# Indirect transfers of a gated cross-attention kernel, issued without their limit-check operand

## The chip, the cores and the metric

The kernel runs on one core of one Trainium2 chip. The metric is the device time of one execution in microseconds (us). The kernel before takes 6575.31 us, the median of three runs (6571.84 to 6575.43).

The core has five engines that run side by side: TensorE (PE in the profile, its weight loads PEld), VectorE (DVE), ScalarE (ACT), GpSimd (POOL) and SyncE (SP), which here issues most of the DMAs. A small q behind a name (POOLq) is the instruction queue of that engine: its register moves, branches and waits.

## The reference

Four layers, each x = x + tanh(gate) * attention(layernorm(x)) and then x = x + tanh(gate) * ffn(layernorm(x)), over 2048 tokens of width 256, with a context of 1601 rows. What matters here are the three places in which rows are picked by computed numbers.

```python
# layer 0, attention: 16 heads, 5 sample points for each; offsets are computed from the query
loc_x = jnp.mod(ref + off + loc, sign_lens[:, None, None, None])
x0 = jnp.floor(ix)
i0 = x0.astype(jnp.int32)          # first of two neighbouring context rows
i1 = i0 + 1
sk = 0.5 * (w0 * _gather_pad0(Kh, i0) + w1 * _gather_pad0(Kh, i1))
sv = 0.5 * (w0 * _gather_pad0(Vh, i0) + w1 * _gather_pad0(Vh, i1))
# softmax over the 5 points, weighted sum of sv
...
# layers 2 and 3, ffn: top 2 of 8 experts for each token (layer 2 adds a shared expert)
sel_w, sel_idx = jax.lax.top_k(routing, TOP_K)
acc = acc + we[:, None] * _ffn(xf, w1, b1, w2, b2)
```

## The kernel before, in words

The tokens lie in 16 tiles (NT) of 128 rows (P), one token for each partition. The kernel is a list of stages; at the end of a stage its engines wait for each other, which the traces show as a drain on line 2207. A stage placed "beside" another with POOL skipped runs on the other four engines only, while POOL is still in a longer one.

**Layer 0, attention.** A stage writes a table (`kv_table`) of 26,624 rows of 64 floats: for a context row and a head, the keys and values of this row and of the next one. Another computes, for each token, 80 table rows (NO = 16 heads x 5 points). The function `gather` (line 1315) then fetches one tile: 80 indirect DMAs (line 1319), each with 128 numbers, one for each partition, so 128 rows of 256 bytes. All are issued by POOL. VectorE works on a tile when its 80 transfers have landed (lines 1257 to 1279, some 22 us a tile).

- Tiles 0 to 8 (`stage_sample_early`): POOL gathers into two buffers in turn, `s_got` and `got_late`. Tile t waits until VectorE has freed the buffer of tile t - 2 (line 1271 frees it). The copy of the next tile's numbers (line 1354) stands ahead of each tile. Beside it the other engines build keys and values for the later layers, quantize weights, scan masks, and sample the tiles.
- Tiles 9 to 15 (`stage_gather_late`): POOL gathers a tile into `got_late`, waits for it, stores it to DRAM (`late_rows`, line 1391, a plain DMA from POOL), and waits for the store. Beside it the other engines carry tiles 0 to 7 through two feed-forward layers and one attention. Then `stage_sample_late` loads the seven tiles back (`m_got`) and samples them.

So line 1319 is executed 16 x 80 = 1280 times.

**Layers 2 and 3, experts** (`stage_expert_ffn`, twice). VectorE computes for each token the two places (`place_i`) of its copies in expert order. POOL scatters the normed rows to `slots_in` (line 2150; 16 tiles x 2 copies = 32 indirect DMAs for each of the two layers). SP waits for all 32 (line 1868) and loads slots of 256 rows with the weights of their expert (lines 1870 and 1871); TensorE computes each slot. Layer 2 has a shared expert, computed on TensorE (lines 1929 and 1937) ahead of the slots. When all is stored, POOL fetches the results (line 2158, again 32 for each layer, four tiles ahead), and VectorE adds them up (lines 2139 and 2141).

The numbers are computed so that they lie inside their tables; no row is skipped in the kernel before. The limit is given as a constant; the program puts it into a register of POOL, with one MOVE ahead of each indirect transfer, under the same line.

Of the kernel before, what the change touches and what calls it, by code (L numbers as in the profile page):

```python
# [23 lines left out]
H = 16  # L24
# [3 lines left out]
MPAD = MT * P  # L28
# [7 lines left out]
SLOT = 256  # L36
SLOTS = 2 * S // SLOT + E - 1
# [1277 lines left out]
def gather(env, pool, got, numbers, arrived):  # L1315

    import concourse.bass as bass
    for j in range(NO):
        pool.indirect_dma_start(out=got[:, j, :], out_offset=None, in_=env.table,  # L1319
                                in_offset=bass.IndirectOffsetOnAxis(ap=numbers[:, j:j + 1].bitcast(env.u32), axis=0),  # L1320
                                bounds_check=MPAD * H - 1, oob_is_err=False).then_inc(arrived, 16)


def sample_buffers(env, keep):
# [8 lines left out]
def stage_sample_early(env, keep, scratch):  # L1333
# [13 lines left out]
    def gpsimd(pool):  # L1347
        pool.sem_inc(got_free, 2)
        pool.tensor_copy(numbers[0][:, :], env.rows[:, 0, :]).then_inc(copied, 1)

        def tile(t, k):
            pool.wait_ge(got_free, t + 1)
            pool.wait_ge(copied, t + 1)
            pool.tensor_copy(numbers[(k + 1) % AHEAD][:, :],
                             env.rows[:, bass_ds(t + 1, 1), :].rearrange("p o n -> p (o n)")).then_inc(copied, 1)
            gather(env, pool, got[k % 2], numbers[k], gathered[k % 2])
        with pool.Fori(0, EARLY // AHEAD, 1) as it:
            for k in range(AHEAD):
                tile(it * AHEAD + k, k)
        for t in range(EARLY // AHEAD * AHEAD, EARLY):  # L1360
            tile(t, t % AHEAD)
# [11 lines left out]
def stage_gather_late(env, keep, scratch):  # L1373

    ahead = scratch.enter_context(env.nc.sbuf_tensor("l_ahead", [P, NO], env.i32))
    zeros = scratch.enter_context(env.nc.sbuf_tensor("l_zeros", [P, NO], env.i32))
    copied, taken, zeroed = env.sem("l_copied"), env.sem("l_taken"), env.sem("l_zeroed")
    gathered, kept = env.gather_sem("l_gathered"), env.gather_sem("l_kept")

    def gpsimd(pool):  # L1380
        pool.memset(zeros[:, :], 0).then_inc(zeroed, 1)
        pool.wait_ge(zeroed, 1)
        pool.tensor_copy(ahead[:, :], env.rows[:, EARLY, :]).then_inc(copied, 1)
        with pool.Fori(0, NT - EARLY, 1) as j:
            pool.wait_ge(copied, j + 1)
            pool.tensor_tensor(env.numbers[:, :], ahead[:, :], zeros[:, :], env.ALU.add).then_inc(taken, 1)
            pool.wait_ge(taken, j + 1)
            pool.tensor_copy(ahead[:, :], env.rows[:, bass_ds(j + (EARLY + 1), 1), :].rearrange("p o n -> p (o n)")).then_inc(copied, 1)
            gather(env, pool, env.got_late, env.numbers, gathered)
            pool.wait_ge(gathered, j * (16 * NO) + 16 * NO)  # L1390
            pool.dma_start(env.late_rows[bass_ds(j * P, P), :], env.got_late[:, :, :].rearrange("p n c -> p (n c)")).then_inc(kept, 16)
            pool.wait_ge(kept, j * 16 + 16)
    return {"pool": gpsimd}
# [387 lines left out]
def stage_expert_ffn(env, keep, scratch, n):  # L1781
# [8 lines left out]
    def sb(name, shape, dt=f32):  # L1790
        return scratch.enter_context(nc.sbuf_tensor(f"e{n}_{name}", shape, dt))

    def sem(name):
        return env.sem(f"e{n}_{name}")
# [11 lines left out]
    FETCH = 4  # L1806
# [11 lines left out]
    place_f, place_i, part = sb("place_f", [P, 2, NT]), sb("place_i", [P, NT, 2], env.i32), sb("part", [P, NT, 2])  # L1818
# [7 lines left out]
    scattered = env.gather_sem(f"e{n}_scattered")  # L1826
# [4 lines left out]
    fetched, mixed = [env.gather_sem(f"e{n}_fetched{k}") for k in range(FETCH)], sem("mixed")  # L1831
# [312 lines left out]
    def gpsimd(pool):  # L2144
        pool.iota(slot_no[:, :], [[1, SLOTS]], base=0, channel_multiplier=0, allow_small_or_imprecise_dtypes=True).then_inc(iota_made, 1)  # L2145
        pool.wait_ge(*ln["y"])
        pool.wait_ge(placed, 1)
        for t in range(NT):
            for k in range(2):
                pool.indirect_dma_start(out=env.slots_in, in_=env.Y[:, t, :], in_offset=None,  # L2150
                                        out_offset=bass.IndirectOffsetOnAxis(ap=place_i[:, t, k:k + 1].bitcast(env.u32), axis=0),
                                        bounds_check=SLOTS * SLOT - 1, oob_is_err=False).then_inc(scattered, 16)
        pool.wait_ge(all_stored, 1)
        for t in range(NT):
            if t >= FETCH:
                pool.wait_ge(mixed, 2 * (t - FETCH) + 2)
            for k in range(2):
                pool.indirect_dma_start(out=got[t % FETCH][:, k, :], out_offset=None, in_=env.slots_out,  # L2158
                                        in_offset=bass.IndirectOffsetOnAxis(ap=place_i[:, t, k:k + 1].bitcast(env.u32), axis=0),
                                        bounds_check=SLOTS * SLOT - 1, oob_is_err=False).then_inc(fetched[t % FETCH], 16)  # L2160

    return {"pe": tensor, "act": scalar, "dve": vector, "sp": sync, "pool": gpsimd}

# [167 lines left out]
```

## Time and profile before

| | |
|---|---|
| median of three runs | 6575.31 us (6571.84 to 6575.43) |
| span of the profiled execution | 5943.9 us |
| difference of the two | 631.4 us |
| indirect transfers | 1280 (L1319) + 64 (L2150) + 64 (L2158) = 1408 |
| POOL busy | 1506.2 us, 25% of the span |
| PE busy | 3795.9 us, 64% of the span |

The span goes from the first to the last instruction of the profiled execution. A time of its own for that execution isn't given beside the span; what the runs take beyond it is the 631.4 us of the table, and lies outside what the trace shows.

### The profile page before, as it was taken

The page shows a single profiled execution, that of the slowest core. Times are in us where ns is not written, and L with a number is a line of the kernel's source. Part 1 is how long each engine was busy: PE and PEld are TensorE (multiplying, and loading weights), DVE is VectorE, ACT ScalarE, POOL GpSimd, SP SyncE. Part 2 cuts the span into 40 slices and gives each one's busy share as a digit, 9 for nine tenths or more (in the row PEclk, how much of TensorE's full clock was granted, in tenths as well). Part 3 has the DMA queues.
Part 4 walks back from the last instruction along what each step waited for, and adds up shares of the span by engine and source line. Part 5 has one row for each costly group of instructions (what it writes and reads, how often), then busy time and mean ns, then how long its engine had stood idle before and what let it go on. Part 6 is the DMA issues. An engine that isn't in the chain of part 4 may idle for free.

```text
span 5943.9 us, 71309 instructions
## 1 busy us (share of the span) xinstructions
PE 3795.9 (64%) x19888; PEld 1731.9 (29%) x19894; DVE 2791.6 (47%) x3817; ACT 1990.8 (33%) x3720; POOL 1506.2 (25%) x1461
## 2 busy tenths in 40 slices
PE   7700410037962013996599969974899999997695
PEld 2300200022321001332133336862222222222485
DVE  3131221276753276776566630013766666673201
ACT  1100100014751001673155621212366666664131
POOL 0767777677767400000000010010000000000202
PEclk9555655557986555998699979986799999999698
DMA  2331311013321211110211111534100111101243
GB/s 83 90 118 24 108 38 24 21 55 106 92 93 39 92 66 48 51 51 20 81 52 47 42 60 65 192 137 117 43 25 25 32 33 33 33 25 32 110 181 135
DMA packets 195461, 403.88 MB, mean 68 GB/s; under 512 B 46405, under 2 KB 130649, under 8 KB 186074
## 3 DMA queue, kind: packets, MB, share of 16 engines
q1 hardware_dynamic: 147114, 323.79, 17.0%
q0 software_dynamic: 48112, 77.16, 4.6%
q8 instruction: 122, 2.00, 0.1%
q14 instruction: 113, 0.93, 0.1%
HBM read 301.77 MB, written 106.10 MB: 69 GB/s over the span
## 4 chain that ended last, share of the span: by engine, by line
PE 47%; POOL 20%; DVE 10%; issue 10%; DMA 7%; ACT 2%; SPq 1%; POOLq 1%; DVEq 1%; ACTq 0%; PEldq 0%
POOL got_late L1319 13%; PE PS L694 13%; PE PS L657 9%; PE PS L675 8%; POOL s_got L1319 6%; PE PS L1959 5%; PE PS L1969 5%; DVE a_maxima L789 3%; ACT a_probs L745 1%; DMA q_parts<-a_parts 1%; PE PS L1929 1%; DMA late_rows<-got_late 1%; PE PS L1937 1%; PE PS L1122 1%; DMA Y<-denominators 1%
## 5 line engine op out<-in xcount | busy, mean ns | idle before, releaser
L789 DVE TENSOR_REDUCE a_maxima<-PS 128x1 f32<-128x1024 f32 (+8 forms) x1696 | 1637.9, 990 | 685.3 <-PE PS L657 468.7
L745 ACT ACTIVATE a_probs<-PS 128x512 f32<-128x512 f32 (+4 forms) x2896 | 1503.3, 572 | 771.7 <-PE PS L675 568.3
L657 PE MATMUL PS<-a_k_max,a_q_max 96*128 96x512 bf16 (+2 forms) x3136 | 913.5, 371 | 153.1 <-DVE a_maxima L789 90.4
L675 PE MATMUL PS<-a_q_exp,a_k_exp 97*128 97x512 bf16 (+4 forms) x2896 | 970.2, 376 | 58.6 <-ACT a_probs L745 30.6
L694 PE MATMUL PS<-a_probs,a_v_head 128*32 128x256 f32 (+4 forms) x7456 | 964.5, 496 | 31.8 <-DVE a_v_head L804 11.2
L2145 POOL IOTA e_slot_no<- 128x23 f32 x2 | 0.3, 162 | 2944.1 <-DVEq L2207 2944.1
L1319 POOL DMA_INDIRECT got_late<-kv_table,numbers x560 | 576.8, 1030 | 171.9 <-issue 171.9
L675 PEld LDWEIGHTS PS<-a_q_exp,a_k_exp 97*128 97x128 bf16 (+1 forms) x2896 | 271.7, 99 | 697.6 <-ACT a_probs L745 442.7
L657 PEld LDWEIGHTS PS<-a_k_max,a_q_max 96*128 96x128 bf16 x3136 | 263.8, 100 | 692.9 <-DVE a_maxima L789 386.6
L1319 POOL DMA_INDIRECT s_got<-kv_table,s_numbers x400 | 428.5, 1071 | 121.9 <-issue 121.9
L1298 PE MATMUL PS<-identity,s_ctx 128*128 128x128 f32 x18 | 6.2, 449 | 668.9 <-DVE s_ctx L1274 668.9
L1319 POOL DMA_INDIRECT got_late<-kv_table,s_numbers x320 | 348.5, 1089 | 96.9 <-issue 96.9
L1959 PE MATMUL PS<-e_slotT,e_w 128*128 128x256 f32 x1280 | 287.2, 383 | 11.7 <-DMA e_w<-in_ew 11.7
L2011 ACT ACTIVATE e_hid<-PS,e_w 128x256 f32<-128x256 f32 x320 | 151.4, 473 | 409.2 <-PE PS L1959 409.2
L694 PEld LDWEIGHTS PS<-a_probs,a_v_head 128*32 128x32 f32 (+1 forms) x7456 | 169.3, 108 | 407.9 <-ACT a_probs L745 241.8
L1969 PE MATMUL PS<-e_w,e_hid 128*128 128x256 f32 x1280 | 283.0, 379 | 1.4 <-ACT e_hid L2011 1.4
L1959 PEld LDWEIGHTS PS<-e_slotT,e_w 128*128 128x128 f32 x1280 | 246.1, 192 | 46.4 <-issue 12.3
L1969 PEld LDWEIGHTS PS<-e_w,e_hid 128*128 128x128 f32 x1280 | 240.2, 190 | 33.1 <-issue 2.2
L2158 POOL DMA_INDIRECT e_got<-slots_out,e_place_i x64 | 64.0, 999 | 711.3 <-SPq L1893 692.4
L1287 ACT ACTIVATE s_weight<-s_score 128x80 f32<-128x80 f32 x9 | 2.4, 269 | 634.9 <-DVE s_score L1266 634.9
L1298 PE MATMUL PS<-identity,m_ctx 128*128 128x128 f32 x14 | 4.8, 447 | 326.4 <-DVE m_ctx L1274 326.4
L1298 PEld LDWEIGHTS PS<-identity,s_ctx 128*128 128x128 f32 x18 | 2.6, 204 | 674.4 <-DVE s_ctx L1274 674.4
(342 smaller groups left out, 3309.9 us busy)
## 6 DMA issues: line engine op xcount, KB each, us to landing
e_w<-in_ew SPq DMA_DIRECT2D x41, 2052.0 KB, 8.1
late_rows<-got_late POOLq DMA_DIRECT2D x7, 2560.0 KB, 7.9
m_got<-late_rows SPq DMA_DIRECT2D x7, 2560.0 KB, 9.2
a_k_max<-k_parts SPq DMA_DIRECT2D x48, 300.2 KB, 3.8
a_k_exp<-k_parts SPq DMA_DIRECT2D x48, 300.2 KB
a_q_max<-q_parts SPq DMA_DIRECT2D x32, 384.0 KB, 3.6
a_q_exp<-q_parts SPq DMA_DIRECT2D x32, 384.0 KB
a_k_max<-k_parts SPq DMA_DIRECT2D x16, 684.2 KB, 5.7
```

Source lines behind the costliest of these rows:

```text
L657: last = pe.matmul(bank[:, b0:b1], q_max[hh][:, P * t:P * (t + 1)], k_max[hh][:, k0 + b0:k0 + b1], start=True, stop=not (lo < hi or masked))
L675: last = pe.matmul(bank[0:rows, q - CH * c:CH], k_exp[hh][:, k0:k0 + rows], q_exp[hh][:, q:CH * (c + 1)], start=True, stop=not (on_diag or ...
L694: last = pe.matmul(sum_bank[32 * c:32 * c + 32, q - SUM * c:SUM], v_head[hh][0:rows, t, :], probs[i % PROB_SLOTS][0:rows, q - at:SUM * (c ...
L745: act.activation(probs[i % PROB_SLOTS][0:rows, q - CH * c:CH], exp_bank[i % EXP_BANKS][0:rows, q - CH * c:CH], ACT.Exp).then_inc(probs_rea ...
L789: dve.tensor_reduce(maxima[hh][:, t, k0 // MAX_COLS:k0 // MAX_COLS + 1], max_bank[s[1] % MAX_SLOTS][:, 0:w], AX.X, ALU.max).then_inc(max_t ...
L1122: pe.matmul(bank, env.CT[:, c, c0:c0 + P], wkv[:, c, :], start=(c == 0), stop=False)
L1319: pool.indirect_dma_start(out=got[:, j, :], out_offset=None, in_=env.table, in_offset=bass.IndirectOffsetOnAxis(ap=numbers[:, j:j + 1].bit ...
L1929: last = pe.matmul(PS[:, f % 4, :], w1[1][:, c, P * f:P * (f + 1)], env.YT[:, c, CH * chunk:CH * (chunk + 1)], start=(c == 0), stop=(c == ...
L1959: last = pe.matmul(PS[:, f % 4, 0:SLOT], w1[k][:, c, P * f:P * (f + 1)], slotT[k][:, c, :], start=(c == 0), stop=(c == DC - 1))
L1969: last = pe.matmul(PS[:, 4 + k, D * j:D * (j + 1)], hid[k][:, f, P * j:P * (j + 1)], w2[k][:, f, :], start=(f == 0), stop=(f == FT - 1))
L2011: act.activation(hid[k][:, f, 0:SLOT], PS[:, f % 4, 0:SLOT], ACT.Gelu_apprx_tanh, bias=b1[k][:, f:f + 1]).then_inc(hid_out, 1)
L2158: pool.indirect_dma_start(out=got[t % FETCH][:, k, :], out_offset=None, in_=env.slots_out, in_offset=bass.IndirectOffsetOnAxis(ap=place_i[ ...
```

## The change

`bounds_check` and `oob_is_err` are left out at all three places. The numbers, tables, semaphores and order stay. The parameter `oob_is_err` so takes its default, which is True, instead of False.

```diff
@@ gather @@
     for j in range(NO):
         pool.indirect_dma_start(out=got[:, j, :], out_offset=None, in_=env.table,
-                                in_offset=bass.IndirectOffsetOnAxis(ap=numbers[:, j:j + 1].bitcast(env.u32), axis=0),
-                                bounds_check=MPAD * H - 1, oob_is_err=False).then_inc(arrived, 16)
+                                in_offset=bass.IndirectOffsetOnAxis(ap=numbers[:, j:j + 1].bitcast(env.u32), axis=0)).then_inc(arrived, 16)
...
@@ stage_expert_ffn, scatter @@
                 pool.indirect_dma_start(out=env.slots_in, in_=env.Y[:, t, :], in_offset=None,
-                                        out_offset=bass.IndirectOffsetOnAxis(ap=place_i[:, t, k:k + 1].bitcast(env.u32), axis=0),
-                                        bounds_check=SLOTS * SLOT - 1, oob_is_err=False).then_inc(scattered, 16)
+                                        out_offset=bass.IndirectOffsetOnAxis(ap=place_i[:, t, k:k + 1].bitcast(env.u32), axis=0)).then_inc(scattered, 16)
...
@@ stage_expert_ffn, fetch @@
                 pool.indirect_dma_start(out=got[t % FETCH][:, k, :], out_offset=None, in_=env.slots_out,
-                                        in_offset=bass.IndirectOffsetOnAxis(ap=place_i[:, t, k:k + 1].bitcast(env.u32), axis=0),
-                                        bounds_check=SLOTS * SLOT - 1, oob_is_err=False).then_inc(fetched[t % FETCH], 16)
+                                        in_offset=bass.IndirectOffsetOnAxis(ap=place_i[:, t, k:k + 1].bitcast(env.u32), axis=0)).then_inc(fetched[t % FETCH], 16)
```

## Rows read from the trace of the kernel before

**Rows 1.** The page: where the chain that ended last lies, by line.

```profile
POOL got_late L1319 13%; PE PS L694 13%; PE PS L657 9%; PE PS L675 8%; POOL s_got L1319 6%; PE PS L1959 5%; PE PS L1969 5%; DVE a_maxima L789 3%; ACT a_probs L745 1%; DMA q_parts<-a_parts 1%; PE PS L1929 1%; DMA late_rows<-got_late 1%; PE P
```

**Rows 2.** Groups of POOL: count, busy us, mean ns, idle us before, releaser.

```profile
L1319 POOL DMA_INDIRECT got_late<-kv_table,numbers x560 | 576.8, 1030 | 171.9 <-issue 171.9
L1319 POOL DMA_INDIRECT s_got<-kv_table,s_numbers x400 | 428.5, 1071 | 121.9 <-issue 121.9
L1319 POOL DMA_INDIRECT got_late<-kv_table,s_numbers x320 | 348.5, 1089 | 96.9 <-issue 96.9
L2158 POOL DMA_INDIRECT e_got<-slots_out,e_place_i x64 | 64.0, 999 | 711.3 <-SPq L1893 692.4 <-issue 11.9 <-DVE X L2141 7.0
```

**Rows 3.** Waits: who waited for what, total us, times, longest us.

```profile
POOL s_numbers L1354 <- DVE s_prod L1271: 20.9, 1, 20.9
...
ACT L1287 <- POOLq L2207: 189.0, 1, 189.0
...
PE PS L1949 <- DMA e_rows_in<-slots_in: 34.8, 2, 31.2
```

**Rows 4.** Stretches of the first 2029 us: length, busy (count) by engine, clock, DMA.

```profile
core 0: us, PE busy (x) PEld busy (x) DVE busy (x) ACT busy (x) POOL busy (x), PEclk, DMA share, GB/s
...
390.00:1168.00 778.00, 90.75 (x216) 50.76 (x216) 149.26 (x149) 32.92 (x74) 608.05 (x567) 0.54 0.16 43
...
1192.00:2029.00 837.00, 433.99 (x3049) 172.55 (x3052) 460.11 (x689) 287.17 (x486) 584.72 (x580) 0.73 0.25 74
```

**Rows 5.** Timeline, POOL and VectorE: start us, us, instruction, [idle before it].

```profile
389.91 0.25 POOL L1354 COPY s_numbers<-rows 128x80 int32 x1 [20.94 <-DVE s_prod L1271]
...
776.65 1.49 DVE L1271 TENSOR_TENSOR s_prod<-s_got,s_weight 128x1280 f32<-128x1280 f32 x1
...
835.02 0.27 POOL L1354 COPY s_numbers<-rows 128x80 int32 x1
835.45 1.02 POOL L1319 DMA_INDIRECT s_got<-kv_table,s_numbers  x1 [0.17 <-issue]
836.77 3.36 POOL L1319 DMA_INDIRECT s_got<-kv_table,s_numbers  x1 [0.30 <-issue]
```

**Rows 6.** The chain that ended last, in order of time: start us, us, what.

```profile
1304.37 2.46 DMA got_late<-kv_table,numbers
1307.63 7.87 DMA late_rows<-got_late
...
3658.70 12.53 PE PS L1937 x58
...
5580.62 0.98 POOL slots_in L2150
5581.91 2.42 DMA slots_in<-Y,e_place_i
5584.97 0.39 SPq L1870
...
5927.24 2.72 DMA e_got<-slots_out,e_place_i
```

**Rows 7.** POOL's instructions by line: duration ns min/median/max, first and last start.

```profile
L1319 POOLq MOVE  x1280: 29/29/38, 149.1 to 1994.6; - x183
L1319 POOL DMA_INDIRECT got_late<-kv_table,numbers x560: 992/997/1973, 1192.8 to 2010.5; - x187
...
L1391 POOL DMA_DIRECT2D late_rows<-got_late x7: 576/578/597, 1307.6 to 2013.6; - x7
...
L2150 POOLq MOVE  x64: 29/29/29, 3544.0 to 5566.2; - x64
L2150 POOL DMA_INDIRECT slots_in<-Y,e_place_i x64: 978/983/1033, 3544.8 to 5581.9; - x64
```

**Rows 8.** The same of line 2150 alone, from 3544 to 3552 us.

```profile
L2150 POOLq MOVE  x14: 29/29/29, 3544.6 to 3551.6; - x14
L2150 POOL DMA_INDIRECT slots_in<-Y,e_place_i x6: 978/978/1033, 3544.8 to 3551.3; - x6
```

**Rows 9.** Timeline of POOL: in a late tile, early in a scatter, and at its end.

```profile
1203.28 1.00 POOL L1319 DMA_INDIRECT got_late<-kv_table,numbers  x1 [0.30 <-issue]
...
3548.72 0.98 POOL L2150 DMA_INDIRECT slots_in<-Y,e_place_i  x1 [0.30 <-issue]
...
5579.33 0.99 POOL L2150 DMA_INDIRECT slots_in<-Y,e_place_i  x1 [0.30 <-issue]
```

## The prediction

> **What bounds the kernel now.** I read the chain of the page first. Its largest single line is 1319, POOL's gathers: 13% for `got_late` and 6% for `s_got`, some 1130 us, though POOL is busy for only a quarter of the span [rows 1]. So the mean busy shares mislead, and the stages have to be read one by one.
>
> The stretch from 390 to 1168 us is 778 us long; POOL is busy for 608.05, VectorE for 149.26, PE for 90.75. From 1192 to 2029 us it is POOL 584.72 of 837, VectorE 460.11, PE 433.99 [rows 4]. What ends last there is in the waits: at the end of the second stretch ACT waits 189.0 us for POOL's drain, so the other engines are done long before; in the first, POOL waits on VectorE only once, 20.9 us, ahead of tile 2 [rows 3]. From then on POOL gathers without a stop, and its pace is the pace of the kernel. Tiles 0 and 1 are gathered before 389.91 us, where POOL waits for a buffer [rows 5]: their 160 gathers are hidden. The other 560 early and 560 late ones are on the path.
>
> In the experts: the last scatter of the second one starts at 5580.62, lands, and SP's load at 5584.97 starts behind it [rows 6]; PE waits 31.2 us for the first slot [rows 3], while 32 scatters take 41 us, so all 32 count. In the first expert stage the scatters begin at 3544.8 [rows 7] and are over after those 41 us, but PE is in the shared expert until 3671 (3658.70 + 12.53) [rows 6], so its 32 are hidden with 85 us to spare. The 64 fetches are on the path: of their 711.3 us of idle time 692.4 are the wait for the experts, and only 7.0 are for VectorE [rows 2], so they run at POOL's own pace up to the last landing at 5927.24 [rows 6].
>
> On the path: 1120 + 32 + 64 = **1216 transfers** of 1408. One takes 997 ns, the median, with 0.30 us of issue before it [rows 7, 9], so 1.30 us: 1216 x 1.30 = 1581 us, 24% of the time. The kernel answers with 1.2 us to each nanosecond of one transfer.
>
> **The change, part by part.** Three things can become cheaper.
>
> *The MOVE.* One of 29 ns goes with each transfer, 1280 under line 1319 [rows 7]. If it stood in POOL's path, it would be worth its 29 ns and some 24 ns more to start. But it is hidden by the body of the transfer: in the first scatters 14 MOVEs are executed while 6 scatters start [rows 8], and the gap ahead of each is 0.30 us all the same [rows 9]. The other end of the scatter says it more plainly: the last MOVE is at 5566.2, the last scatter at 5581.9 [rows 7]; a dozen scatters run with no MOVE between them, and the gap is still 0.30 [rows 9]. I take 0 for the MOVE. If that cover were gone, it would cost 53 ns a transfer.
>
> *The 0.30 us gap.* It is the same for gathers and scatters, with and without a MOVE [rows 9]; nothing shows that it depends on the operand. The smallest is 0.17 us, behind a copy [rows 5], so a gain ends at 0.13; I know of no row for a loss and give it the 0.05 of a MOVE. I take 0, as the regular rows do.
>
> *The body.* No transfer of the trace goes without the limit, so this is bounded by neighbours. The plain DMA of line 1391, also built by POOL for 128 partitions, takes 578 ns; a gather takes 997 [rows 7]. Reading 128 numbers, making addresses of them and comparing them is all in the 419 ns between, and the comparison is between 0 and 419. Below nothing: the default `oob_is_err=True` asks for a report where before a row was skipped, which could lengthen the body; I see no row that excludes it and put the end at 30 ns more. Within the 419 I lean to the low end: of four kinds of work there a comparison is the smallest. The nearest row for a small step of such a body is the difference of scatter (983) and gather (997), 14 ns, for the same 128 numbers [rows 7]. A limit has to be applied both to what is read and to what is written, so I take two such steps, **28 ns**. That is my choice between ends far apart.
>
> Sum: 1216 x 28 ns = 34.0 us off the path. The 192 hidden transfers give nothing. The span goes from 5943.9 to 5909.9 us; the runs take 631.4 us more than the span of the profile, which I leave as it is: **6541.3 us**, 0.5% less than 6575.31.
>
> What is late next? In the late stretch the other engines have 189.0 us of slack over 560 gathers [rows 3], 0.34 us for each, so nothing takes over. In the early one POOL starts tile 6 at 835.02, and the buffer of tile 4 is free at 778.1 (776.65 + 1.49) [rows 5]: 57 us over the 320 gathers of tiles 2 to 5, so a gain of up to 0.18 us for each is passed on in full. The fixed part of a late tile, 2.46 us until the last gather has landed and 7.87 for the store [rows 6], stays. So does what VectorE costs POOL: a gather that meets a long VectorE instruction takes 3.36 us instead of 1.0 [rows 5], by which the means of 1030 to 1089 ns lie above 997 [rows 2]; these delays come from VectorE's 22 us a tile and don't shrink with the body.
>
> Measured against the price of one transfer as a whole, the trace and a page part ways. A gather occupies POOL for 997 ns, and 80 of them follow each other, while the landing of 2.46 us shows once for each tile [rows 6, 7]; so here the building is paid each time and completion once. The Trainium skill, page "DMA: Bandwidth & Descriptors", section "Anatomy of one DMA — SWDGE (gpsimd) path", says that the fixed 2 us of such a DMA are mostly the receipt of the write and that descriptor generation is small. By that rule a lighter building would change nothing. It is the first rival below, reached there from rows alone.
>
> **The rivals.**
>
> *Nothing changes.* The body does the comparison anyway, against some largest number, or beside other work; or the program puts a limit in by itself, so that the change doesn't do what it says. For it: the body is very even (992 to 997 for more than half of the gathers), as of code with no decisions for each number [rows 7]. Against it: a comparison is work, and a body of 1 us for 128 numbers is long enough to hold it. It gives 6575.3 us, give or take 0.2%.
>
> *The comparison is dear.* A decision for each of the 128 numbers, one by one, is a third of the 419 ns, 140 ns: 1216 x 140 = 170 us, 6405 us. It stays under the 0.18 us at which the early buffers bind [rows 5]. Against it: the same evenness. The Trainium skill, "GPSIMD Engine Reference", section "Elementwise — side-by-side cycle accounting", gives about 12 cycles an element for data-dependent branching; an estimate from that page, with 128 numbers spread over eight cores at 1.2 GHz, is 160 ns. No row here shows such a branch.
>
> *The MOVE is in the path after all*, since 53 ns of 304 are its own: 1216 x 53 = 64 us, 6511 us. Rows 8 and 9 speak against it.
>
> *Slower: the default error mode.* With `oob_is_err=True` and no limit given, the body checks each transfer against the table's own size and prepares a report; this is in POOL's body at lines 1319, 2150 and 2158. It decides from 11 ns a transfer on (1216 x 11 = 13 us, 0.2%); at 28 ns more, two steps as above, it costs 34 us: 6609 us. For it: the diff drops this operand too. Against it: it would be more work with less information.
>
> **How the numbers follow.** I call 0.2%, 13 us, the least that a measurement of this kernel can tell from no change; that is 11 ns a transfer. Chances: the forecast (a body shorter by 11 to 90 ns) 0.38, dear comparison 0.10, MOVE in the path 0.05, nothing 0.34, slower 0.13. So faster 0.53, same 0.34, slower 0.13. The forecast alone reaches from 6466 (90 ns: 109 us) to 6562. For 8 in 10 I go from 6466, which leaves out the dear comparison, to 6598, 19 ns a transfer on the slow side, which leaves out about 8 in 100 above it.
>
> **What would show it.** The MOVEs under 1319, 2150 and 2158 must be gone; if they are there, the operand is too. The gap stays 0.30 us: if it falls to 0.25, the MOVE was in it. The median body of a gather falls from 997 to about 969 ns, of a scatter from 983 to 955; the seven plain DMAs keep 578. POOL's stretch in each late tile shortens by 80 x 28 ns = 2.2 us, and ACT's wait of 189.0 us falls by about 16. I would be wrong if the body is unchanged, if it grows, or if another engine's waits grow by what POOL gives.

## The result, and the profile after

| | before | changed |
|---|---|---|
| median of 16 runs each | 6573.64 us (6568.77 to 6587.4) | 6563.66 us (6553.68 to 6569.94) |
| span of the profiled execution | 5943.9 us | 6556.2 us |
| a gather: body, median | 997 ns | 947 ns |

The ratio is 0.9983 with the interval 0.9976 to 0.9990: 0.17% or 10 us less, where 34 us were forecast. It lies in the range, but by the prediction's own bound of 0.2% it is no change. The cause is not a small effect on the gather. The body is shorter by 50 ns, more than the 28 forecast.

The changed kernel, groups of POOL (count, busy us, mean ns, idle us before), then the same lines' durations (ns min/median/max, first and last start):

```profile
L1319 POOL DMA_INDIRECT got_late<-kv_table,numbers x560 | 541.6, 967 | 178.2 <-issue 178.2
L1319 POOL DMA_INDIRECT s_got<-kv_table,s_numbers x400 | 410.3, 1026 | 122.1 <-issue 122.1
...
L1319 POOL DMA_INDIRECT got_late<-kv_table,numbers x560: 942/947/1719, 1405.1 to 2191.2; - x187
...
L1390 POOL DMA_DIRECT2D late_rows<-got_late x7: 578/583/599, 1507.6 to 2194.3; - x7
...
L2149 POOL DMA_INDIRECT slots_in<-Y,e_place_i x64: 970/974/1018, 4147.2 to 6195.3; - x64
L2156 POOL DMA_INDIRECT e_got<-slots_out,e_place_i x64: 949/949/987, 4587.2 to 6539.5; - x64
```

Beside [rows 2] and [rows 7]: the MOVEs are gone, the plain DMA is within 5 ns of what it was, a gather went from 997 to 947 ns, a scatter only from 983 to 974. With 1216 transfers on the path, as the prediction counted, that would be near 60 us. 10 were measured. And the span doesn't fit at all: it is 612 us *longer* than the span of before. Page of the changed kernel, busy tenths in 40 slices:

```profile
span 6556.2 us, 69907 instructions
...
PE   7240121002110596138956997799389999998496
...
POOL 1715764766766200000000000100100000000101
```

Before, the same two rows of the page:

```profile
PE   7700410037962013996599969974899999997695
...
POOL 0767777677767400000000010010000000000202
```

In the trace before, POOL gathers in slices 2 to 14, and PE has 3 to 9 tenths in slices 9 to 12, in the midst of them: the work beside the gathers is done beside them. In the changed kernel PE has 0 to 2 tenths in slices 4 to 13, as long as POOL gathers, and its dense part begins behind them. So either the change makes the other engines stand still for 600 us, and the timed runs don't show it, or the first trace isn't of an execution like the timed ones. The latter took 631.4 us more than that trace, "which I leave as it is".

### The profile page after: what moved, and what is told of

Its sections match the earlier page's. It is cut to its first block, busy times and chain, and to the rows that moved or that the text cites. A ratio compares the mean times of both kernels' runs of the same rounds, so it can differ in the third digit from the quotient of the medians.

```text
span 6556.2 us, 69907 instructions
## 1 busy us (share of the span) xinstructions
PE 3836.3 (59%) x19894; PEld 1740.1 (27%) x19894; DVE 2792.2 (43%) x3817; ACT 1992.3 (30%) x3720; POOL 1419.4 (22%) x1461
## 4 chain that ended last, share of the span: by engine, by line
PE 48%; issue 16%; DVE 11%; another core or an unknown queue 8%; DMA 5%; POOL 4%; SPq 4%; ACT 3%; DVEq 1%; POOLq 0%; ACTq 0%; PEldq 0%
PE PS L694 13%; PE PS L657 9%; PE PS L675 9%; PE PS L1958 4%; PE PS L1968 4%; DVE a_maxima L789 3%; POOL s_got L1319 2%; SPq L372 2%; ACT a_probs L745 2%; POOL got_late L1319 1%; DMA q_parts<-a_parts 1%; PE PS L1936 1%; PE PS L1928 1%; PE PS L721 1%
## 5 line engine op out<-in xcount | busy, mean ns | idle before, releaser
L1319 POOL DMA_INDIRECT got_late<-kv_table,numbers x560 | 541.6, 967 | 178.2 <-issue 178.2
L1319 POOL DMA_INDIRECT s_got<-kv_table,s_numbers x400 | 410.3, 1026 | 122.1 <-issue 122.1
L1319 POOL DMA_INDIRECT got_late<-kv_table,s_numbers x320 | 318.7, 996 | 111.0 <-issue 111.0
L326 PE MATMUL PS<-CT,kv_wk 128*128 x96 | 67.6, 866 | 200.9 <-issue 109.9
```

The lines of the kernel that those rows point to most:

```text
L326: last = pe.matmul(env.PS[:, k, 0:width], weight[:, c, P * half:P * (half + 1)], source[:, c, bass_ds(chunk * width + first, width)], star ...
```

## The experiments

In the comparisons below, "before" is the kernel before, timed on the same chip beside the kernel that it is compared with, and times are medians.

**Is the first trace like the timed runs?** The kernel before, once more, unchanged.

> The kernel before, unchanged, profiled once more, since the span of the changed kernel (6556.2 us) equals its time and that of the kernel before (5943.9 us) does not. Theory A (the profiled execution of before ran without delays that its timed executions have): this trace has a span of some 6570 us, PE, ACT and VectorE stand still for hundreds of us between 150 and 2200 us while POOL gathers, POOL is done before the others, and the gathers are for the most part not on the path. Theory B (POOL sets the pace until 2029 us, as predicted, and the gain was given back elsewhere): the span is some 5944 us again, or the extra time lies outside the gathers' stretch.

Measured: 6571.83 us in a run of its own (before: 6578.91 over 15 runs), with a span of 6570.1 us. Wherever one execution has both, its time exceeds its span by 1.7 us, never by hundreds. Its page:

```profile
span 6570.1 us, 71309 instructions
...
PE   7240112001222396137966998799389999998496
...
POOL 1715774767676400000000000100100000000101
```

That is the picture of the changed kernel. So the change has no part in it, and the trace of [rows 1 to 9] shows the same program under another condition. I call the one of 6575 us **the long condition** and the one of 5944 us **the short condition**. All comparisons from here on are made within one of them; which one an experiment met could not be chosen.

**Where do the 631 us lie?** One kind of work beside POOL is enough to see it: line 789, VectorE's maxima of the attention of tiles 0 to 7, 256 in all. First window: POOL's late gathers; second: from their end to the start of the load of `m_got` (length us, VectorE busy in this line, count, clock, DMA share, GB/s). Before, first trace:

```profile
1193.00:2011.00 818.00, 247.33 (x256) 0.74 0.24 72
```

The kernel before in the long condition:

```profile
1423.00:2235.00 812.00, 54.91 (x56) 0.53 0.18 55
2235.00:2646.00 411.00, 193.73 (x200) 0.89 0.13 43
```

In the short condition all 256 are done before the last late gather, and 18 us later the stage is over. In the long one 56 are, and the other 200 need 411 us more. There POOL does not set the end of the late stretch; the others do, and they set it with work that they could have done earlier. What they do meanwhile, in the changed kernel, in order of time (start us, us, instruction, [idle before it]):

```profile
2002.76 1.23 DVE L789 TENSOR_REDUCE a_maxima<-PS 128x1 f32<-128x1024 f32 x1 [30.74 <-remote]
...
2008.05 0.63 PE L675 MATMUL PS<-a_q_exp,a_k_exp 97*128 97x512 bf16 x1
...
2030.14 0.60 ACT L745 ACTIVATE a_probs<-PS 128x512 f32<-128x512 f32 x1 [23.98 <-remote]
...
2030.79 0.61 PE L675 MATMUL PS<-a_q_exp,a_k_exp 97*128 97x512 bf16 x1 [22.10 <-issue]
...
2036.36 0.76 DVE L789 TENSOR_REDUCE a_maxima<-PS 128x1 f32<-128x577 f32 x1 [32.38 <-remote]
```

PE ends a matmul at 2008.68, ACT takes its result at 2030.14, and nothing that the trace shows lies between; POOL issues a gather each 1.25 us all the while. The waits of this kernel (who, line, releaser: total us, times, longest) name it "remote", a releaser that isn't in the trace:

```profile
DVE a_maxima L789 <- remote: 350.4, 27, 32.8
```

The trace of the short condition has no such wait in this line. In the long condition engines that issue none of these DMAs stand still for up to 33 us at a time in this line while POOL issues them. The Trainium skill, page "DMA: Bandwidth & Descriptors", section "Anatomy of one DMA — SWDGE (gpsimd) path", calls the descriptor generation of such transfers small. The traces don't bear that out for gathers: the body takes 947 ns of POOL each time, one behind the other.

By what way POOL's gathers and the standstills are tied no run here shows. Two ways can be looked for in the traces of the kernel before. The late gathers of the short condition, and then those of the long one (queue, kind: packets, MB, share of 16 engines over 818 and 812 us):

```profile
q0 software_dynamic: 18728, 34.06, 14.0%
q8 instruction: 11, 0.18, 0.1%
q14 instruction: 10, 0.08, 0.0%
```

```profile
q0 software_dynamic: 18732, 34.07, 13.8%
q8 instruction: 7, 0.11, 0.1%
q14 instruction: 8, 0.07, 0.0%
```

The same packets of POOL's queue keep the DMA engines busy as long in both, so the transfers themselves aren't slower. And 15 packets of instructions arrive in the long one, fewer than its 25 waits on "remote" in line 789 alone, so a standstill isn't the loading of a packet of code each time. What else the engines wait for stays unknown.

**Does the time still follow the number of gathers?** Half of the 80 gathers of a tile, in the kernel before.

```diff
-    for j in range(NO):
+    for j in range(NO // 2):
```

> The kernel before with 40 of the 80 gathers of each tile; the other half of the buffers is filled with zeros once, so half of the sample points are left out of the first attention. The gather work of POOL falls by 560 us on the path of the prediction. Theory B: POOL sets the pace, so the time falls by at least 300 to 570 us (the others' 189 us of slack in the late stretch and some 100 in the early one bind). Theory A with delays that have nothing to do with the gathers: it falls by under 100 us. Theory A with delays that come from the gathers themselves: it falls by several hundred us, and in the trace the standstills of PE and ACT between 150 and 2200 us shrink with the gathers.

Measured: 5804.51 us, ratio 0.8833 (0.8818 to 0.8847), 774 us less for 640 gathers, 1.21 us for each. By its size that fits both theories that tie the time to the gathers; the windows tell them apart. Late stretch and rest (PE, PEld, VectorE, ACT, POOL busy; clock; DMA):

```profile
980.00:1425.00 445.00, 103.07 (x424) 47.00 (x425) 158.66 (x267) 41.44 (x66) 297.02 (x298) 0.54 0.24 75
1425.00:1856.00 431.00, 347.37 (x2625) 127.44 (x2627) 299.32 (x420) 246.22 (x420) 0.58 (x1) 0.90 0.14 44
```

Late gathers 445 us instead of 812, that is 367 us for 280 gathers, 1.31 us for each; the rest 431 instead of 411. In 55% of the time the others had done 70% as many steps (39 of the 256 maxima, against 56), so the rest grew by 20 us only. A gather that is left out is paid back nearly in full even where POOL isn't last. Four gathers more for each tile, in the changed kernel:

```diff
-    for j in range(NO):
+    for j in range(ALL):
+        n = j % NO
```

(`ALL` is `NO + 4`; buffers and waits follow.)

> The changed kernel with 84 instead of 80 gathers for each tile (4 repeated ones into a spare part of the buffer): POOL has 14 x 4 x 1.25 = 70 us more on the path of the prediction, about what the lighter body took from it (1120 x 50 ns = 56 us). Theory B: 60 to 75 us slower than the changed kernel, so some 50 us slower than the kernel before. Theory A: the same factor as for the change, in which 56 us of POOL's time gave some 7 us: 5 to 15 us slower than the changed kernel, so within 10 us of the kernel before.

Measured: 6642.23 us, ratio to before 1.0103 (1.0087 to 1.0119), 79 us above the changed kernel's 6563.66, which was timed at another time. Where POOL isn't the bound I had expected 5 to 15, where it is 60 to 75; it is a miss for both, and near the second. The late gathers took 819 us (787 before the addition) and the rest 453 (439): each of the 28 late ones costs over 1.1 us in POOL and half a microsecond more behind it. So the number of gathers is dear, while 50 ns off each of them have brought 10 us.

**Is it the MOVE, the limit or the error mode?** The limit's register loaded once for each tile instead of ahead of each gather:

```diff
+    limit = env.nc.alloc_register(pool.engine)
+    env.nc.reg_mov(limit, MPAD * H - 1)
...
-                                bounds_check=MPAD * H - 1, oob_is_err=False).then_inc(arrived, 16)
+                                bounds_check=limit, oob_is_err=False).then_inc(arrived, 16)
```

> The kernel before, with the limit of the 80 gathers of a tile put into a register once instead of 80 times; the operand stays. This takes away the MOVEs and leaves the comparison. If the shorter body (997 to 947 ns) comes from the comparison: the body stays 997 ns and the gap 0.30 us, and the time stays within 3 us of the kernel before or so. If it comes from the MOVE or from fewer instructions in POOL's queue: the body or the gap falls, and a part of the 10 us comes back.

Measured: 6570.04 us, 0.9992 (0.9983 to 1.0001), no difference. The time could hardly show one, since a cheaper gather gives little in this condition; the bodies and gaps below can. And the other half, the limit kept and only `oob_is_err=False` left out at all three places:

> The kernel before with oob_is_err left at its default, True, and the limit in place. It separates the limit from the error mode. If the 50 ns come from the comparison: the body of a gather stays 997 ns (some ns more for the report). If they come from the mode in which a row is skipped: it is 947 ns, with the MOVEs still there.

Measured: 6564.37 us in a single run, too little for a verdict on its time. Bodies of the two (ns min/median/max), the register loaded once first:

```profile
L1321 POOL DMA_INDIRECT got_late<-kv_table,numbers x560: 992/997/1769, 1420.7 to 2226.4; - x187
```

The default mode with the limit kept:

```profile
L1319 POOL DMA_INDIRECT got_late<-kv_table,numbers x560: 1006/1010/1782, 1417.9 to 2234.5; - x187
```

Taking the MOVEs away leaves the body at 997, and the gap stays at 0.30 us:

```profile
1431.18 0.99 POOL L1321 DMA_INDIRECT got_late<-kv_table,numbers  x1 [0.30 <-issue]
```

The default mode with a limit makes the body 13 ns longer. So the MOVE has no part in the 50 ns, and the mode, as long as there is a limit, works against it. In the default mode, leaving the limit out takes the body from 1010 to 947, 63 ns; the 50 of the change are these 63 less the 13 of the mode. A kernel without a limit and with the old mode wasn't run, so whether the mode matters without a limit isn't known.

**Which of the gathers count?** The limit left out for tiles 0 to 8 only, and for 9 to 15 only; the experts keep it in both.

```diff
-            gather(env, pool, got[k % 2], numbers[k], gathered[k % 2])
+            gather(env, pool, got[k % 2], numbers[k], gathered[k % 2], False)
...
-            gather(env, pool, env.got_late, env.numbers, gathered)
+            gather(env, pool, env.got_late, env.numbers, gathered, True)
```

(`gather` passes the two operands only where its new last argument is True; the second kernel has the two values exchanged.)

> The kernel before, with the limit left out of the gathers of tiles 0 to 8 alone. Theory A1, from the traces of the kernel before (again), the changed one and one with half the gathers: of the early gathers those of tiles 2, 3, 6, 7 and 8 are on the path (400 x 50 ns = 20 us), while in the late stretch the other engines hardly get on as long as gathers are issued, and what a lighter body gains there is lost again. So this kernel should gain 12 to 20 us on the kernel before, as much as the whole change (10 us) or more. Rival A2 (the gain is spread evenly over all gathers on POOL's path, only smaller): 720/1280 of 7 us, 4 us.

> The kernel before, with the limit left out of the gathers of tiles 9 to 15 alone. Theory A1: POOL's late stretch is 25 us shorter, and the rest of the stage behind it is longer by as much, some 435 to 440 us instead of 411; the time is within 5 us of the kernel before, or some us slower. Rival A2: 3 us faster. Rival B: 25 us faster.

Measured, before 6578.75: early alone 6554.56 us, ratio 0.9964 (0.995 to 0.9977); late alone 6583.53 us, 1.0010 (1.0001 to 1.0019). The early part gives 24 us (15 to 33). The late one gives nothing, and by the interval it even costs a little, 1 to 12 us. The windows of line 789 show why. The changed kernel, then early alone, then late alone:

```profile
1405.00:2192.00 787.00, 34.76 (x35) 0.50 0.20 54
2192.00:2631.00 439.00, 213.83 (x221) 0.91 0.14 44
```

```profile
1405.00:2214.00 809.00, 54.88 (x56) 0.52 0.18 54
2214.00:2625.00 411.00, 193.89 (x200) 0.89 0.14 44
```

```profile
1422.00:2210.00 788.00, 34.75 (x35) 0.51 0.18 54
2210.00:2652.00 442.00, 213.93 (x221) 0.90 0.13 43
```

Lighter late gathers end POOL's stretch 22 to 25 us sooner, 787 against 809 and 812 us. But the others then have 35 of their 256 steps done instead of 56, and the rest takes 28 to 31 us longer. The counts come back exactly: 35 with a gather each 1.25 us (two kernels), 56 with one each 1.30 (three: before, the register loaded once, early alone). Each stretch is from one trace; the three with 1.30 us are 807 to 812 us long and the two with 1.25 us 787 and 788, so the 20 us between the groups are more than what traces of one group differ by. What POOL gives, the others take. The start of the late stretch, on the other hand, keeps the early gain: 1405 us instead of 1422.

**Would a pause in the gathers free the others?** The changed kernel, in which POOL waits for the landing after each 20 gathers.

```diff
+        if j % GROUP == GROUP - 1 and j < NO - 1:
+            pool.wait_ge(arrived, base + 16 * (j + 1))
+            pool.sem_inc(past, 1)
```

> The changed kernel, where POOL waits after each 20 gathers until they have landed; that adds three waits of some 2.7 us a tile, about 8 us a tile and 110 us on POOL's path. If the other engines are held up by gathers that pile up behind each other, they get on in these pauses and at the start of each group: the standstills shrink, and the time falls in spite of the pauses, by up to several hundred us. If they are held up by something that each gather does, pauses of 8% of the time help little: 50 to 110 us slower than the changed kernel.

Measured: 6571.61 us, 0.9988 (0.9979 to 0.9997), by the ratios 3 us above the changed kernel. I had expected either a gain of up to several hundred us or a loss of 50 to 110; it is neither. Its two windows:

```profile
1418.00:2243.00 825.00, 162.70 (x660) 59.66 (x661) 184.45 (x297) 65.17 (x105) 548.55 (x578) 0.52 0.18 54
2243.00:2643.00 400.00, 316.82 (x2389) 117.68 (x2391) 275.83 (x391) 224.60 (x381) 0.58 (x1) 0.89 0.14 44
```

POOL's stretch grows by 38 us and the rest shrinks by 39: the same exchange, the other way. So I tried to make the gaps wide, three and five small copies on POOL behind each gather, and, for the indirect form itself, 80 plain DMAs of fixed rows in its place:

```diff
+        fill(env, pool, ahead, rows, copied, j)
```

```diff
-        pool.indirect_dma_start(out=got[:, j, :], out_offset=None, in_=env.table,
-                                in_offset=bass.IndirectOffsetOnAxis(ap=numbers[:, j:j + 1].bitcast(env.u32), axis=0)).then_inc(arrived, 16)
+        pool.dma_start(got[:, j, :], env.table[P * j:P * (j + 1), :]).then_inc(arrived, 16)
```

> The changed kernel, with three small copies on POOL behind each gather (one of them makes the next tile's numbers, column by column, in place of one copy a tile; two go to a spare tile). It lengthens the period of a gather from 1.25 to some 1.45 us and nothing else. Estimate from the late stretch of the traces so far: behind the last gather of a tile the other engines stand still for some 9 us more at a period of 1.30 us with 80 gathers, over 12 us at 1.25, 4.5 us at 1.30 with 40 gathers; each gather looks as if it left behind work of about 1.41 us for something that the others need. Theory A3: from a period of 1.41 us on nothing piles up, the others run as in the first trace of the kernel before, and the late stretch ends with POOL's gathers (R near 20 instead of 439 us): the time falls to some 6200 us or lower, though POOL's gathers take 1120 x 0.2 = 224 us longer. Rival: each gather holds up the others by a fixed share whatever its pace: POOL's 224 us come on top less what the others do in them, so some 6600 to 6750 us.

> The same with five copies behind each gather, a period of some 1.65 us. Theory A3: the others are as free as with three copies, POOL's gathers set the pace, so about 0.2 us x 1120 = 220 us slower than with three. Rival: slower than with three by less, since the others do more meanwhile, but neither below 6570 us.

> The changed kernel with a plain DMA from POOL, of the same 128 rows of 256 bytes, in place of each gather (rows of fixed numbers, so the first attention samples wrong rows; the amount of work is the same). It asks whether the standstills come with the indirect form. If they come with any stream of small transfers from POOL: they are there as before or worse, as the body is shorter (near 0.6 us). If they come with the indirect form: PE, ACT and VectorE run freely between 150 and 2200 us and the time is far below 6000 us.

These ran in the short condition: before took 5946.62 us, and the three 6370.15 (1.0708), 6724.06 (1.1305) and 5359.55. In it the others have no standstill that could be taken away, and the copies only lengthen POOL's path. So these kernels say nothing on the standstill. The first and the third ran twice more, on two other chips:

> The kernel with three copies behind each gather once more. On a chip without standstills: 7% slower, 6370 us, as measured. On a chip with them it tests theory A3: if the others only stand still where gathers follow each other faster than something can digest (estimate: 1.41 us each), then with a period of 1.6 us they run freely and the time is 6370 us as well, 200 us faster than the kernel before. Rival: 6700 us or more.

> Plain DMAs from POOL in place of the gathers once more (fixed rows, so the first attention samples wrong rows). Without standstills 5360 us, as measured. On a chip with them: 5360 us if they come with the indirect form; some 300 us and more above it if they come with any stream of small transfers from POOL.

> The kernel with three copies behind each gather, sent once more to reach a chip with standstills. There: 6370 us by theory A3 (the others are free where gathers come slowly enough), 6600 us or more by its rival. On a chip without them it says nothing new: 6370 us.

> Plain DMAs from POOL in place of the gathers (fixed rows, so the first attention samples wrong rows), sent for a chip with standstills: 5360 us if these come with the indirect form, some 300 us and more above it if they come with any stream of small transfers from POOL.

Measured: 6370.32 and 6371.07 us with the copies, 5367.37 and 5363.44 with plain DMAs, before 5948.74 and 5950.76: the short condition each time. They repeat the first times to 0.02% and 0.15%, and leave the question where it was.

**Is the prediction's own account right where it was read?** The short condition is the one of its rows, so the changed kernel and its two halves belong there:

> The changed kernel once more. The last chip ran the kernel before in 5946.6 us, as long as its first trace, and the chips before it in 6579. So there are chips with the standstills and chips without. Where the kernel before takes 5946 us, the sum of the prediction should hold with the body's real size: 1216 transfers, 1152 of them gathers and fetches x 50 ns and 32 scatters x 10 ns, some 58 us: 5888 us, 1.0% faster. Where it takes 6575: 10 us faster, as measured first.

> Limit left out of the gathers of tiles 0 to 8 alone, once more. On a chip without standstills: 560 x 50 ns = 28 us faster than the kernel before, half of what the whole change brings. On a chip with them: 24 us faster, more than the whole change, as measured before.

> Limit left out of the gathers of tiles 9 to 15 alone, once more. On a chip with standstills it is up to 5 us slower than the kernel before, as measured; on a chip without them the late stretch is on POOL's path and it is 560 x 50 ns = 28 us faster.

(The first of these texts counts 1152 gathers and fetches; with the 64 fetches it is 1184, 1120 + 64, which makes its 58 us 59.5: 1184 x 50 ns + 32 x 9 ns.)

Measured: all of it 5892.28 us, 0.9904 (0.9887 to 0.9920), 56.5 us less; early alone 5923.17, 0.9954 (0.9937 to 0.9971), 25.6 less; late alone 5921.84, 0.9950 (0.9933 to 0.9966), 28.9 less (20 to 40 by the interval). The changed kernel here, its line 789 in the late stretch, its gathers and ACT's wait for POOL:

```profile
1165.00:1956.00 791.00, 247.27 (x256) 0.75 0.25 75
```

```profile
L1319 POOL DMA_INDIRECT got_late<-kv_table,numbers x560: 940/944/1994, 1165.2 to 1955.3; - x187
```

```profile
ACT L1287 <- POOLq L2204: 162.3, 1, 162.3
```

All 256 steps are done under the gathers, and of the 189.0 us of [rows 3] 162.3 are left: the slack shrinks by 27 us, what 560 gathers give at 48 ns, and no other engine becomes late. In this condition the late gathers are worth their full 28.9 us; in the other they were worth nothing.

The starts and ends that the comparisons rest on, in us of each trace:

| kernel | condition | late gathers start | end | load of `m_got` starts | line 789 done by the end |
|---|---|---|---|---|---|
| before | short | 1193 | 2011 | 2029 | 256 |
| changed | short | 1165 | 1956 | 1974 | 256 |
| before | long | 1423 | 2235 | 2646 | 56 |
| changed | long | 1405 | 2192 | 2631 | 35 |
| early alone | long | 1405 | 2214 | 2625 | 56 |
| late alone | long | 1422 | 2210 | 2652 | 35 |
| half the gathers | long | 980 | 1425 | 1856 | 39 |
| four more | long | 1443 | 2262 | 2715 | 30 |
| paced | long | 1418 | 2243 | 2643 | 62 |
| register once | long | 1421 | 2227 | 2638 | 56 |
| default mode, limit kept | long | 1418 | 2236 | 2636 | 61 |

## Why the prediction was half right

- **The MOVE is worth nothing, the gap stays 0.30 us.** Right in the number, and for the gathers by another way. The body hides the MOVE in the first scatters, as [rows 8] say. In a train of gathers it doesn't:

```profile
L1319 POOL DMA_INDIRECT got_late<-kv_table,numbers x3: 993/997/999, 1202.0 to 1204.6; - x3
L1319 POOLq MOVE  x3: 29/29/29, 1203.0 to 1205.6; - x3
```

  The first of these gathers is over at 1203.0, the MOVE starts there, and the next gather starts at 1203.28 [rows 9]. So the MOVE lies in the gap, and the gap is 0.30 us all the same: with the MOVEs taken away it stays, as shown above, and in the changed kernel too:

```profile
2000.69 0.94 POOL L1319 DMA_INDIRECT got_late<-kv_table,numbers  x1 [0.30 <-issue]
```

  So the rival that puts the MOVE in the path falls.
- **The body, 28 ns.** The step had the right sign and the wrong size: 50 ns for gathers and fetches (997 to 947, 999 to 949), 9 for scatters (983 to 974). The neighbour that I chose, the 14 ns between a scatter and a gather, measured something else; that a limit costs two such steps no run shows. The neighbour could not have told me more: with the limit the gather is the longer of the two by 14 ns, without it the shorter by 27, so the limit's price depends on the form. The rival of the dear comparison (140 ns) and that of no change in the body fall with this.
- **The error mode.** It had a case: with the limit kept it lengthens the body by 13 ns, in place of my 28. Without the limit it is in the changed kernel, whose body is shorter in sum.
- **1216 transfers on the path.** Right in the condition of the rows: 1184 x 50 + 32 x 9 ns = 59.5 us, and 56.5 were measured, 28.9 of them in the 560 late gathers (28.0 by the sum). With 50 in place of 28 ns, that working gives the changed kernel of that condition to 3 us. The 50 is the long condition's; in the short one the median body fell by 53 ns (997 to 944) and the mean by 44 to 48, with the longest late gathers as long as before (1.97 and 1.99 us). By the busy times, which hold both, the fall on the path is 26.9 us for the late gathers, 25.8 for 560 of the 720 early ones, 3.4 for the fetches and 0.4 for half of the scatters, 56.5 in all; that it is the measured time to a tenth is chance, as the interval is 48 to 67 us. One reading was off by an instruction: the last scatter starts at 5581.9 [rows 7], and 5580.62 is the one before it; the sum doesn't depend on it.
- **The step that failed: "the runs take 631.4 us more than the span of the profile, which I leave as it is".** I took them as lying outside of what the trace shows, and so summed on the trace as if the timed runs had its waits. They lie inside: in the long condition the kernel before spans 6570.1 us, 626 more, and the load of `m_got` is 617 of them later. 230 arise ahead of the late gathers (1423 instead of 1193) and 393 behind their end (411 instead of 18), while POOL's late stretch itself is 6 us shorter. In that condition POOL isn't what ends the late stretch, so 560 of the 1216 transfers are worth nothing or less: 28 us that the sum at 50 ns has and the runs don't. The wait on which the sum rested, ACT's 189.0 us for POOL, isn't there. In its place the kernel before has:

```profile
ACT L1287 <- DVEq L2207: 51.7, 1, 51.7
```

  With it goes the answer to "what is late next". The prediction's last sign of being wrong, that another engine's waits grow by what POOL gives, is what came true.
- **The early stretch, in the long condition.** The prediction let 560 early gathers count. Between the start of tile 2 and the end of tile 8 there, POOL waits on VectorE for long:

```profile
POOL s_numbers L1353 <- DVE s_prod L1271: 268.1, 2, 185.5
```

  Before it was 266.9 us in that condition, against 20.9 in one wait in [rows 3]. That wait swallows the gain of the tiles ahead of it. The late stretch starts at 1405 instead of 1423 us, 18 us sooner, which is the price of about 360 to 400 gathers at 50 ns (tiles 2, 3, 6, 7 and 8 make 400). The runs gave 24 for the early part alone (15 to 33 by the interval), so the count of tiles is argued and not shown. Early and late part together make 19 us of those two kernels' times, and 10 were measured for the whole; the intervals are wide enough for both.
- **The sum again, in the long condition.** Early 18 us less, late gathers 25 less, rest 28 more: 15 us less at the load of `m_got` (2646 to 2631), and 13.9 at the end of the span (6570.1 to 6556.2). The runs say 10 (7 to 16 by the interval). The experts' 64 fetches and 32 scatters, 3.5 us by their bodies, are too small to be seen in this.
- **That the time lies in the range is luck.** Two errors stand against each other: the body fell by 50 ns and not 28, and 10 us are the price of only some 200 gathers at 50 ns and not of 1216 transfers. The rival "nothing changes", to which I gave 0.34, has the time right and the mechanism wrong: the body did change.
- **The rival that POOL isn't the bound** was missing among mine. I had looked for an engine that becomes late and found 189.0 us of slack. The trace was of the condition in which that slack exists.

Two things stay open. *What sets the condition*: the kernel before was in the long one on a chip and in the short one on the same chip 27 minutes later, so it doesn't belong to the chip or to the kernel; no more is known. *How POOL's gathers hold the others*: their number matters (half of them, four more), the nanoseconds of the late ones don't, and the steps that the others get done grow with the time between two gathers: 30 and 35 steps at 1.25 us, 56 at 1.30, 61 at 1.31 (the default mode with the limit kept). That would fit something that costs about 1.4 us for each gather and drains behind POOL, an estimate from how long the others stay still behind the last gather of a tile. It is argued and not shown: behind the last tile they take up work 9.6 us later in the changed kernel, 7.9 before and 4.8 with half the gathers, but 1.7 us later with early alone. The kernels meant to test it met the other condition, so whether the number, the spacing or the indirect form decides is untested.

The best kernel depends on the condition: in the long one it is early alone (6554.56 us, 24 less than before beside it), in the short one the whole change (5892.28 us, 56.5 less).

## What to carry to other kernels

Hold the span of a trace against the timed runs before anything is summed on it; 631 us between them are a tenth of the kernel, and must be looked for *inside* the stretches, with a second trace of the unchanged kernel as the first experiment. A cheaper instruction on the engine that looks like the bound pays only where that engine ends the stretch: here the same 28 us of late gathers were worth 28.9 us in one condition and nothing in the other. Leaving out the limit and the mode of an indirect gather of 128 rows takes 50 ns of 997 off POOL's body, and the MOVE that loads the limit costs nothing beside it.

## What was not expected of the hardware

- The same program on the same chip took 6579 us at one time (15 runs, 6563 to 6583) and 5949 at another (7 runs, 5946 to 5954); in the first, PE, ACT and VectorE stand still for up to 33 us at a time while POOL issues indirect transfers.
- In the late stretch of the long condition the granted clock is 0.50 to 0.54 of full speed, so at its lower level, 1.2 of 2.4 GHz, for nearly all of the time; in the same stretch it was 0.73 in the short condition, where PE is busy for 434 of 837 us [rows 4], against 112 of 787 in the changed kernel. In the rest behind POOL's end it is 0.89 to 0.91.
- A plain DMA in the place of each gather has a median body of 534 ns instead of 944 and almost no gap ahead of it (1.2 us before 880 of them, against 0.30 us before each gather). It makes the kernel some 530 us shorter than the changed one in the short condition (5363 against 5892; three single runs, 5359.55 to 5367.37). It leaves out the choice of rows, so the kernel computes something else; as an estimate it says how much could at most be had from making the 128 addresses more cheaply:

```profile
L1319 POOL DMA_DIRECT2D got_late<-kv_table x880 | 468.0, 597 | 1.2 <-issue 1.2
...
L1319 POOL DMA_DIRECT2D got_late<-kv_table x880: 534/534/1292, 190.7 to 1165.2; - x176
```
